# Expert outputs scattered to their tokens' rows, and a combination that loads rows in order

## The chip, the cores and the metric

The kernel runs on one core of a Trainium2 chip. The metric is the device time of one execution in microseconds (us), the median of several runs. The core has five engines that run side by side and wait for each other through semaphores: TensorE (PE in the profile; PEld is its weight load), VectorE (DVE), ScalarE (ACT), GpSimd (POOL) and SyncE (SP), which here issues most DMAs. GpSimd can issue DMAs too, among them the indirect ones, which take a row number per partition.

## What is computed

Two layers of a gated cross-attention network on x of 16 x 256 tokens with 256 numbers each. The change touches only the last block, a mixture of experts with 8 routed experts, of which each token takes 2, and 2 shared ones:

```python
gates = xf @ router_w + router_b
topv, topi = jax.lax.top_k(gates, TOP_K)                 # TOP_K = 2
probs = jax.nn.softmax(topv, axis=-1)
comb = jnp.einsum('nke,nk->ne', jax.nn.one_hot(topi, E), probs)
h = gelu(jnp.einsum('nd,edh->enh', xf, w1) + b1[:, None, :])
y = jnp.einsum('enh,ehd->end', h, w2) + b2[:, None, :]
moe_out = jnp.einsum('ne,end->nd', comb, y)              # 4096 tokens, D = 256, H = 512
shared_out = (jnp.einsum('snh,shd->nd', sh, sw2) + sb2.sum(0)) / S
out = x + tanh(g) * (shared_out + moe_out)
```

## The kernel before

Four phases follow each other; the last, `phase_moe`, has three stages. Every matmul in float32 precision is done as three passes over a high and a low part (`three_passes`, lines 32 to 34), so each operand has a `_hi` and a `_lo` tile: a copy makes the high part, a subtraction the low one.

**Routing** (`moe_route`): 16 chunks of 256 tokens. The layer norm gives `z`; the gates give each token its two experts and, by a count with matmuls, a place in each expert's region of the DRAM tensor `d_z_rows`. GpSimd scatters each token's `z` row to its two places with 64 indirect DMAs (line 2502). Small tables on VectorE say for each of the 39 tiles of 256 rows which expert it belongs to and at which row it starts (`tiles_at`), and for each token and choice where its result will stand (`pos`). The first shared expert runs in this stage too.

**Expert tiles** (`moe_experts`): a software pipeline over 39 tiles (`PAIR_TILES`), written as one order of parts for all engines:

```python
ORDER = (("load_w", 3), ("begin", 1), ("split_w", 2), ("load", 4), ("turn_in", 2), ("first", 1), ("second", 0))
```

In step n an engine does its share of `load_w` for tile n+3, of `begin` for tile n+1, and so on. SyncE loads weights (`load_w`) and stores results (`second`, line 2980). GpSimd copies the weights' high part (`split_w`, a small COPY at line 2993 and the CAST at 2994) and loads the tile's rows (`load`, line 3003). VectorE makes the weights' low part (`split_w`, line 3059), the low part of the turned tokens (`turn_in`, line 2941), the low parts of the hidden values (`begin` and `first`, line 3068) and the sum with the bias (`second`, `ys`, line 3089). TensorE transposes the tile (`turn_in`, line 2951, four matmuls) and multiplies 24 + 24 times. Steps 3 to 34 are a loop in the program of two steps per turn; each engine runs its own instructions in order. A buffer number `u` is the tile's number modulo 2. `load` on GpSimd is:

```python
alone(pool, zt_done, i - 1, passed)
row = pool.value_load(M.tiles_at[:, 1, bass.ds(i, 1)], min_val=0, max_val=(E + 1) * S.ROWS - TOK)
pool.dma_start(z[u][:], z_rows[bass.ds(row, TOK), :].rearrange("(t p) d -> p t d", p=P)).then_inc(z_loaded[u], 16)
```

`alone` waits for a semaphore; `value_load` reads a row number into a register of the sequencer (line 3002). Semaphores that matter: `zt_done` counts transposed tiles, `w_hi_done` and `w_lo_done` the split weights, `gelu_lo` the low parts of hidden values, `y_copied` the finished `ys`, `stored` the DMAs that have emptied a `ys` buffer.

**Combination** (`moe_combine`): 16 chunks again. The second shared expert is computed (`hidden`, `outputs`), and each chunk's 512 expert results are gathered from `d_y_rows` by four indirect DMAs on GpSimd (line 3205) into `rows`, weighed and added to `x_all` by VectorE (`weigh`, line 3244), whose sum with the shared output goes out. VectorE's order is hidden of chunk n, `weigh(n - 1)`, outputs of chunk n - 1.

## Time and profile before

| | |
|---|---|
| median of 3 runs | 1186.05 us (1181.33 to 1189.27) |
| span of the profiled execution | 1181.6 us |
| what lies around the span (median less span) | 4.4 us |
| routing stage | to about 825 us |
| expert tiles | about 825 to 1066 us |
| combination | 1066 us to the end |
| TensorE busy in the whole span | 1096.0 us (93%) |
| VectorE, ScalarE, GpSimd busy | 874.2, 698.7, 442.7 us |

The profiled execution has no other time of its own than its span, from its first to its last instruction. The median of the runs stands beside it, and the difference is what a forecast made in the span's time has to be given back. Busy time doesn't say what bounds a stage; that is read from who waits for whom in it.

### The profile page before, as it was taken

How to read it: one execution, taken by the hardware profiler on the slowest of the kernel's cores; microseconds unless marked ns; L12 is line 12 of the kernel's file. 1: busy time of each engine (PE TensorE's matmuls, PEld its weight loads, DVE VectorE, ACT ScalarE, POOL GpSimd, SP SyncE). 2: the span in 40 equal slices, each digit the busy share in tenths (PEclk: the TensorE clock that was granted, in tenths of full speed). 3: DMA queues.
4: the chain of work that ended last, by engine and by line, in shares of the span. 5: the costliest groups of instructions: out<-in, count | busy, mean ns of one | idle time of the engine just before them, and what ended most of it. 6: DMA issues, size and time to landing. Idle time of an engine off the chain costs nothing. (4 is left out here: it accounts for less than half of the span.)

```text
span 1181.6 us, 28194 instructions
## 1 busy us (share of the span) xinstructions
PE 1096.0 (93%) x9246; PEld 943.8 (80%) x9247; DVE 874.2 (74%) x1984; ACT 698.7 (59%) x1584; POOL 442.7 (37%) x577
## 2 busy tenths in 40 slices
PE   6599988999988999999998798899999999998998
PEld 4366667898976777777775598888999999997987
DVE  8799997766667888888887386476676666664665
ACT  3599975646543676667766543266655555563453
POOL 4278865522201110212100037563423332324664
PEclk9689999999998999999999977889999999998999
DMA  9666621000035454554531167665455455544664
GB/s 320 198 233 218 220 71 54 1 0 0 0 56 123 97 127 88 105 106 88 127 76 38 39 219 256 246 227 201 162 178 171 161 174 169 178 152 143 217 197 140
DMA packets 98895, 164.81 MB, mean 139 GB/s; under 512 B 12140, under 2 KB 73420, under 8 KB 96620
## 3 DMA queue, kind: packets, MB, share of 16 engines
q1 hardware_dynamic: 88988, 136.75, 39.3%
q0 software_dynamic: 9104, 26.49, 6.8%
q8 instruction: 56, 0.92, 0.3%
q10 hardware_dynamic: 704, 0.30, 0.1%
q14 instruction: 43, 0.35, 0.1%
HBM read 103.76 MB, written 33.69 MB: 116 GB/s over the span
## 5 line engine op out<-in xcount | busy, mean ns | idle before, releaser
L1924 DVE TENSOR_REDUCE c_mx<-d_bank 128x2 f32<-128x512 f32 x256 | 164.3, 685 | 14.1 <-PE d_bank L2078 13.6
L1839 ACT ACTIVATE c_probs<-c_t 128x512 f32<-128x512 f32 x248 | 134.7, 598 | 25.1 <-PE c_t L2104 24.3
L3037 ACT ACTIVATE d_g_full<-d_bank,d_e_bias 128x256 f32<-128x256 f32 x156 | 77.2, 495 | 99.9 <-PE d_bank L34 99.9
L32 PE MATMUL d_bank<-de_zt_hi,d_e_hi 128*128 128x256 f32 x312 | 91.8, 294 | 2.4 <-DVE de_zt_lo L2941 2.4
L33 PE MATMUL d_bank<-de_zt_lo,d_e_hi 128*128 128x256 f32 x312 | 88.4, 283 | 0.0
L34 PE MATMUL d_bank<-d_w_hi,d_g_lo 128*128 x312 | 88.2, 283 | 0.0
L33 PE MATMUL d_bank<-d_w_lo,d_g_hi 128*128 x312 | 88.2, 283 | 0.0
L32 PE MATMUL d_bank<-d_w_hi,d_g_hi 128*128 x312 | 88.1, 283 | 0.0
L34 PE MATMUL d_bank<-de_zt_hi,d_e_lo 128*128 128x256 f32 x312 | 87.9, 282 | 0.0
L1765 POOL CAST c_ct_hi<-c_c_raw 128x512 fp32r<-128x512 f32 x15 | 9.2, 611 | 205.4 <-PE c_misc L34 205.4
L3205 POOL DMA_INDIRECT d_w_lo<-d_y_rows,d_pos x64 | 66.6, 1040 | 51.2 <-ACT d_g_hi L3218 19.8
L32 PE MATMUL d_bank<-d_s_hi,d_g_hi 128*128 128x256 f32 x256 | 76.9, 300 | 3.2 <-DVE d_g_lo L3237 1.8
L33 PE MATMUL d_bank<-d_s_lo,d_g_hi 128*128 128x256 f32 x256 | 75.8, 296 | 2.5 <-issue 2.5
L3038 ACT ACTIVATE d_g_hi<-d_bank,d_e_bias 128x256 fp32r<-128x256 f32 x156 | 77.9, 500 | 0.0
L34 PE MATMUL d_bank<-d_s_hi,d_g_lo 128*128 128x256 f32 x256 | 75.7, 296 | 1.7 <-issue 1.7
L3068 DVE TENSOR_TENSOR d_g_lo<-d_g_full,d_g_hi 128x256 fp32r<-128x256 f32 x156 | 70.6, 490 | 7.4 <-ACT d_g_hi L3038 5.3
L3089 DVE TENSOR_TENSOR de_ys<-d_bank,de_out_bias 128x512 f32<-128x512 f32 x39 | 27.0, 692 | 60.3 <-PE d_bank L34 58.2
L2104 PEld LDWEIGHTS c_t<-c_qt,c_kt 50*128 50x128 f32 x496 | 37.2, 185 | 43.0 <-ACT c_probs L1839 21.1
L1504 PE MATMUL b_y<-b_w,b_g_hi 128*128 128x288 f32 x256 | 70.3, 301 | 0.3 <-DVE b_g_lo L1337 0.3
L2116 PE MATMUL c_o<-c_probs,c_va 128*32 128x256 f32 x1024 | 68.5, 385 | 1.0 <-ACT c_probs L1839 1.0
L1505 PE MATMUL b_y<-b_w,b_g_lo 128*128 128x288 f32 x256 | 68.9, 296 | 0.0
L2502 POOL DMA_INDIRECT d_z_rows<-dr_z,dr_pos_i x56 | 57.4, 1025 | 30.3 <-ACT d_g_hi L2544 15.4
(430 smaller groups left out, 3803.1 us busy)
## 6 DMA issues: line engine op xcount, KB each, us to landing
d_e_raw<-in_w SPq DMA_DIRECT2D x39, 514.0 KB, 3.7
a_mb<-a_maxima SPq DMA_DIRECT2D x15, 1024.0 KB, 7.5
d_w_hi<-d_zt_kept SPq DMA_DIRECT2D x26, 512.0 KB
d_y_rows<-de_ys SPq DMA_DIRECT2D x39, 256.0 KB, 2.1
d_z_in<-d_z_rows POOLq DMA_DIRECT2D x37, 256.0 KB, 3.6
c_kt<-c_k_hi SPq DMA_DIRECT2D x64, 128.0 KB, 3.1
c_qt<-c_q_hi SPq DMA_DIRECT2D x64, 128.0 KB, 3.7
d_zt_kept<-d_w_hi SPq DMA_DIRECT2D x20, 256.0 KB
```

Source lines behind the costliest of these rows:

```text
L32: tensor.matmul(out, lhs_hi, rhs_hi, start=start, stop=False)
L33: tensor.matmul(out, lhs_hi, rhs_lo, start=False, stop=False)
L34: return tensor.matmul(out, lhs_lo, rhs_hi, start=False, stop=stop)
L1504: pe.matmul(y[t][:, 0:WIDE], g_hi[:, m, cols], w2[:, m, :], start=(m == 0), stop=False)
L1505: return pe.matmul(y[t][:, 0:WIDE], g_lo[:, m, cols], w2[:, m, :], start=False, stop=(m == KF - 1))
L1839: act.activation(probs[h % PR][:], t_bank(n, p, k), ACT.Exp).then_inc(exp_done, 1)
L1924: dve.tensor_reduce(mx[n % 2][:, :, k, p:p + 1], s_ps[h % SB], AX.X, ALU.max).then_inc(max_done, 1)
L2116: mm = pe.matmul(o_ps[OSLOT * i:OSLOT * (i + 1), g % 2, :], va[n % R][:, j, h, :], probs[(n * H + h) % PR][:, j, :], start=(j == 0), stop= ...
L3037: act.activation(g_full[:, m, :], hid[m][:, 0:TOK], ACT.Gelu, bias=bias[u][:, m:m + 1]).then_inc(gelu_full, 1)
L3038: act.activation(g_hi[u][:, m, :], hid[m][:, 0:TOK], ACT.Gelu, bias=bias[u][:, m:m + 1]).then_inc(gelu_hi, 1)
L3068: dve.tensor_tensor(g_lo[u][:, m, :], g_full[:, m, :], g_hi[u][:, m, :], ALU.subtract).then_inc(gelu_lo, 1)
L3205: pool.indirect_dma_start(rows[n % RR][:, t * TOP + k, :], None, y_rows, bass.IndirectOffsetOnAxis(ap=M.pos[:, T * n + t, k:k + 1], axis=0 ...
```

## The change

The expert tiles no longer store their results in the order of the tiles. Each `z` row in DRAM is two numbers longer (258 instead of 256): the number of the pair row where its result belongs, plus one, and the token's first expert. The tile's rows bring both along. VectorE works out, in `turn_in`, the row in `d_y_rows` for each of the tile's 256 results (`to_row`): the token's number times 2, plus 0 or 1 by whether this tile's expert is the token's first; padding rows go to spare rows. GpSimd then writes `ys` with two indirect DMAs per tile (`scatter`), a step later than SyncE stored it. In the combination the results of a chunk lie in the order of the tokens, and SyncE loads them with one plain DMA per chunk; GpSimd has no part in it. The `z` load stays on GpSimd and gets a second wait. `share_bias` moves ahead of GpSimd's pipeline, and the loops of VectorE and GpSimd hold four steps per turn.

```diff
 class RoutedRows:
+    D = 256
+    WIDE = D + 2
...
-    z_rows = nc.dram_tensor("d_z_rows", [(S.E + 1) * S.ROWS, S.D], F32, kind="Internal").ap()
-    y_rows = nc.dram_tensor("d_y_rows", [S.PAIR_TILES * S.TOK, S.D], F32, kind="Internal").ap()
+    z_rows = nc.dram_tensor("d_z_rows", [(S.E + 1) * S.ROWS, S.WIDE], F32, kind="Internal").ap()
+    y_rows = nc.dram_tensor("d_y_rows", [S.PAIRS + S.PAIR_TILES * S.TOK, S.D], F32, kind="Internal").ap()
...
         pool.memset(above[:], 1.0).then_inc(pool_ready, 1)
-        pool.memset(zeros[:], 0.0).then_inc(zeros_set, 1)
+        pool.memset(zeros[:, :, 0:D], 0.0).then_inc(zeros_set, 1)
+        pool.memset(zeros[:, :, D:D + 1], 2.0 * (S.PAIRS + S.PAIR_TILES * TOK)).then_inc(zeros_set, 1)
+        pool.memset(zeros[:, :, D + 1:], -1.0).then_inc(zeros_set, 1)
+        pool.iota(M.spare_rows[:], pattern=[[TOK, S.PAIR_TILES], [P, T]], base=S.PAIRS, channel_multiplier=1,
+                  allow_small_or_imprecise_dtypes=True).then_inc(tokens_set, 1)
+        for first, count in ((0, routed.TILES), (routed.TILES, TILES - routed.TILES)):
+            pool.iota(z_cols(first, count, D), pattern=[[2 * P, count], [0, 1]], base=2 * P * first + 1, channel_multiplier=2,
+                      allow_small_or_imprecise_dtypes=True).then_inc(tokens_set, 1)
...
         def mark(g):
             step(dve.tensor_copy(top_f[:], top_i[:, :, 0:TOP]))
+            begun = max(0, routed.TILES - GT * g)
+            if begun > 0:
+                dve.tensor_copy(z_cols(GT * g, begun, D + 1), top_i[:, 0:begun, 0:1])
+            step(dve.tensor_copy(z_cols(GT * g + begun, GT - begun, D + 1), top_i[:, begun:, 0:1]))
...
-        def past_regions():
-            for e in range(1, E):
-                dve.tensor_scalar(past_region[:, e], pos_all[:], float(e * S.ROWS), base_step[:, e - 1:e], ALU.is_ge, ALU.mult)
...
-                    dve.tensor_tensor(pos_all[:], pos_all[:], past_region[:, e], ALU.subtract)
...
-        def store(i, u):
+        def load_late(i, u):
...
-            sync.wait_ge(y_copied, i + 1)
-            sync.dma_start(y_rows[bass.ds(i * TOK, TOK), :].rearrange("(t p) d -> p t d", p=P), ys[u][:]).then_inc(stored[u], 16)
...
-        def load(i, u):
+        def load(i, r):
+            u = r % 2
             if prepared(i):
                 return
             alone(pool, zt_done, i - 1, passed)
+            alone(pool, rows_known, i - 1, passed)
             row = pool.value_load(M.tiles_at[:, 1, bass.ds(i, 1)], min_val=0, max_val=(E + 1) * S.ROWS - TOK)
             pool.dma_start(z[u][:], z_rows[bass.ds(row, TOK), :].rearrange("(t p) d -> p t d", p=P)).then_inc(z_loaded[u], 16)
-            if isinstance(i, int) and i == AHEAD:
-                share_bias()
+
+        def scatter(i, r):
+            alone(pool, rows_known, i + 1, passed)
+            alone(pool, y_copied, i + 1, passed)
+            for t in range(T):
+                pool.indirect_dma_start(y_rows, bass.IndirectOffsetOnAxis(ap=to_row[r][:, t:t + 1], axis=0), ys[r % 2][:, t, :],
+                                        None).then_inc(stored[r % 2], 16)
...
-        pipeline(pool, S.PAIR_TILES, ORDER, {"split_w": split_w, "load": load})
+        share_bias()
+        pipeline(pool, S.PAIR_TILES, (("split_w", 2), ("load", 4), ("scatter", -1)), {"split_w": split_w, "load": load, "scatter": scatter}, per=OR)
...
+        def turn_in(i, r):
+            u = r % 2
             if not turned_before(i):
                 turn_dve(dve, i, u)
+            if prepared(i):
+                dve.wait_ge(M.z_in_loaded[u], 16)
+            else:
+                dve.wait_ge(z_loaded[u], before_last(i, u))
+            after(dve, rows_known, i)
+            dve.tensor_tensor(chosen[:], z[u][:, :, D + 1], M.tile_expert[:, bass.ds(i, 1)].broadcast_to([P, T]), ALU.is_equal).then_inc(chosen_done, 1)
+            dve.wait_ge(chosen_done, 2 * i + 1)
+            after(dve, stored[u], 2 * before_last(i, u) - 16 * T)
+            dve.tensor_tensor(chosen[:], z[u][:, :, D], chosen[:], ALU.subtract).then_inc(chosen_done, 1)
+            dve.wait_ge(chosen_done, 2 * i + 2)
+            dve.tensor_tensor(to_row[r][:], chosen[:], M.spare_rows[:, bass.ds(i, 1), :].rearrange("p i t -> p (i t)"), ALU.min).then_inc(rows_known, 1)
...
+    pairs = y_rows[0:S.PAIRS, :].rearrange("(t p k) d -> p t k d", p=P, k=TOP)
...
+        def load_rows(n):
+            after(sync, weighed, T * TOP * (n - RR + 1))
+            sync.dma_start(rows[n % RR].rearrange("p (t k) d -> p t k d", t=T), pairs[:, T * n:T * (n + 1)]).then_inc(gathered[n % RR], 16)
...
-                for k in range(TOP):
-                    pool.indirect_dma_start(rows[n % RR][:, t * TOP + k, :], None, y_rows,
-                                            bass.IndirectOffsetOnAxis(ap=M.pos[:, T * n + t, k:k + 1], axis=0)).then_inc(gathered[n % RR], 16)
```

```order
L2993 COPY d_e_bias<-d_e_raw 128x4
L2994 CAST d_e_hi<-d_e_raw 128x1024
L46 REGISTER_ALU
L3002 ISA
L3002 TENSOR_LOAD d_tiles_at
L3002 ISA x2
L3003 ISA
L3003 DMA d_z_in<-d_z_rows 128x2x256
```

The same step of GpSimd in the changed kernel:

```order
L3016 COPY d_e_bias<-d_e_raw 128x4
L3017 CAST d_e_hi<-d_e_raw 128x1024
L46 REGISTER_ALU
L3027 ISA
L3027 TENSOR_LOAD d_tiles_at
L3027 ISA x2
L3028 ISA
L3028 DMA d_z_in<-d_z_rows 128x2x258
L3034 DMA d_y_rows<-de_ys,de_to_row 18176x256 x2
```

Two indirect DMAs stand between the load and the next step's copies, and the row number is read behind one more wait.

VectorE in the same loop before, from the weights' low part (d_e_lo) by the turned tokens' (de_zt_lo) to the first of three low parts of hidden values (d_g_lo):

```order
L3059 TENSOR_TENSOR d_e_lo<-d_e_raw,d_e_hi 128x1024
L2940 REGISTER_ALU
L2941 TENSOR_TENSOR de_zt_lo<-d_bank,de_zt_hi 128x512
L3066 REGISTER_ALU
L3068 TENSOR_TENSOR d_g_lo<-d_g_full,d_g_hi 128x256
```

The same piece of VectorE in the changed kernel:

```order
L3091 TENSOR_TENSOR d_e_lo<-d_e_raw,d_e_hi 128x1024
L2964 REGISTER_ALU
L2965 TENSOR_TENSOR de_zt_lo<-d_bank,de_zt_hi 128x512
L3100 REGISTER_ALU
L3102 ISA
L3102 TENSOR_TENSOR de_chosen<-d_z_in,d_tile_expert 128x2
L3103 ISA
L40 ISA
L3105 TENSOR_TENSOR de_chosen<-d_z_in,de_chosen 128x2
L3106 REGISTER_ALU
L3107 ISA
L3107 TENSOR_TENSOR de_to_row<-de_chosen,d_spare_rows 128x2
```

Three operations on two numbers per partition have come between, the last of which raises `rows_known`.

GpSimd at the start of the stage before, where the first load of a tile's rows stands ahead of the shared bias:

```order
L3002 TENSOR_LOAD d_tiles_at
L3002 ISA x2
L3003 ISA
L3003 DMA d_z_in<-d_z_rows 128x2x256
L3011 TENSOR_TENSOR de_out_bias<-de_out_bias 128x256
L3013 TENSOR_SCALAR de_out_bias<-de_out_bias 128x256
L3020 TENSOR_TENSOR de_out_bias<-de_out_bias 128x256 x4
```

And in the changed kernel, where it stands behind:

```order
L3041 TENSOR_TENSOR de_out_bias<-de_out_bias 128x256
L3043 TENSOR_SCALAR de_out_bias<-de_out_bias 128x256
L3050 TENSOR_TENSOR de_out_bias<-de_out_bias 128x256 x4
L3027 TENSOR_LOAD d_tiles_at
L3027 ISA x2
L3028 ISA
L3028 DMA d_z_in<-d_z_rows 128x2x258
```

The six operations on the bias have changed places with the load.

## Rows read from the trace of the kernel before

**Rows 1.** The page's first line.

```profile
span 1181.6 us, 28194 instructions
```

**Rows 2.** Busy time by stretch: expert loop, combination; then clock, DMA share, GB/s.

```profile
838.60:1052.80 214.20, 214.20 (x1810) 214.20 (x1810) 145.33 (x245) 121.56 (x312) 66.35 (x105) 1.00 0.53 176
1066.00:1182.00 116.00, 100.34 (x770) 97.86 (x768) 66.69 (x150) 50.08 (x128) 66.57 (x64) 0.92 0.55 172
```

**Rows 3.** The chain's shares: expert loop, then combination.

```profile
by line: PE d_bank L33 31.2%; PE d_bank L34 31.1%; PE d_bank L32 31.1%; PE d_bank L2951 6.8%
...
by line: PE d_bank L34 29.2%; PE d_bank L33 28.0%; PE d_bank L32 27.9%; issue 8.8%; another core or an unknown queue 1.2%; ACT d_g_full L3217 0.4%; DVE x_all L3256 0.4%; ACT d_g_hi L3218 0.4%; DVE d_g_lo L3237 0.4%; ACTq L2269 0.3%; DVEq L3
```

**Rows 4.** TensorE's transposes: timeline of three tiles, and the line's summary.

```profile
830.16 0.60 PE L2951 MATMUL d_bank<-ident,d_z_in 128*128 128x128 f32 x4
...
842.49 0.60 PE L2951 MATMUL d_bank<-ident,d_z_in 128*128 128x128 f32 x4
...
928.73 0.60 PE L2951 MATMUL d_bank<-ident,d_z_in 128*128 128x128 f32 x4
...
L2951 PEld LDWEIGHTS d_bank<-ident,d_z_in x156: 138/140/226, 818.2 to 1052.2; 128*128 128x128 f32 x156
```

**Rows 5.** Busy time by stretch in the combination; columns as in rows 2.

```profile
1082.00:1086.00 4.00, 1.68 (x5) 1.35 (x5) 0.42 (x1) 0.31 (x1) 2.27 (x3) 0.50 0.39 113
```

**Rows 6.** GpSimd's gathers in the combination: the line's summary, then the timeline.

```profile
L3205 POOL DMA_INDIRECT d_w_lo<-d_y_rows,d_pos x64: 942/1008/1222, 1070.1 to 1169.9; - x64
...
1071.41 0.98 POOL L3205 DMA_INDIRECT d_w_lo<-d_y_rows,d_pos  x1 [0.30 <-issue]
1072.69 0.95 POOL L3205 DMA_INDIRECT d_w_lo<-d_y_rows,d_pos  x1 [0.30 <-issue]
1073.94 0.95 POOL L3205 DMA_INDIRECT d_w_lo<-d_y_rows,d_pos  x1 [0.30 <-issue]
```

**Rows 7.** Timeline of GpSimd in the expert loop.

```profile
929.59 0.18 POOL L2993 COPY d_e_bias<-d_e_raw 128x4 f32<-128x4 f32 x1 [4.10 <-DMA d_e_raw<-in_w]
929.72 1.04 POOL L2994 CAST d_e_hi<-d_e_raw 128x1024 fp32r<-128x1024 f32 x1
931.04 0.71 POOL L3003 DMA_DIRECT2D d_z_in<-d_z_rows  x1 [0.29 <-issue]
```

**Rows 8.** Timeline of VectorE in the expert loop.

```profile
929.81 1.23 DVE L3068 TENSOR_TENSOR d_g_lo<-d_g_full,d_g_hi 128x256 fp32r<-128x256 f32 x1
930.95 1.21 DVE L3059 TENSOR_TENSOR d_e_lo<-d_e_raw,d_e_hi 128x1024 fp32r<-128x1024 f32 x1
932.09 0.68 DVE L2941 TENSOR_TENSOR de_zt_lo<-d_bank,de_zt_hi 128x512 fp32r<-128x512 f32 x1
932.69 1.08 DVE L3068 TENSOR_TENSOR d_g_lo<-d_g_full,d_g_hi 128x256 fp32r<-128x256 f32 x3
```

**Rows 9.** Timeline of VectorE, chained small operations of the routing's tables.

```profile
804.08 0.19 DVE L2691 TENSOR_TENSOR dr_tab<-dr_tab,dr_past 1x39 f32<-1x39 f32 x1
804.30 0.17 DVE L2692 TENSOR_SCALAR dr_tab<-dr_tab 1x39 f32<-1x39 f32 x1
```

**Rows 10.** Summaries: row-number reads, z loads (ns min/median/max, first and last start).

```profile
L3002 POOLq TENSOR_LOAD <-d_tiles_at x37: 285/289/572, 819.0 to 1040.9; - x37
L3003 POOL DMA_DIRECT2D d_z_in<-d_z_rows x37: 715/717/788, 820.5 to 1042.1; - x37
```

**Rows 11.** Timeline of GpSimd, start of the expert stage.

```profile
824.01 2.80 POOL L3020 TENSOR_TENSOR de_out_bias<-de_out_bias 128x256 f32<-128x256 f32 x4
```

**Rows 12.** Timeline of TensorE: matmuls at half the clock.

```profile
1088.35 0.41 PE L32 MATMUL d_bank<-d_w_hi,d_sw_hi 128*128 128x256 f32 x1
1088.56 0.41 PE L33 MATMUL d_bank<-d_w_hi,d_sw_hi 128*128 128x256 f32 x1
```

**Rows 13.** Timeline of VectorE: the last `ys`, the first weighing.

```profile
1066.89 0.69 DVE L3089 TENSOR_TENSOR de_ys<-d_bank,de_out_bias 128x512 f32<-128x512 f32 x1 [1.06 <-PE d_bank L34]
...
1076.70 1.87 DVE L3244 SCALAR_TENSOR_TENSOR x_all<-d_w_lo,d_prob,x_all 128x256 f32<-128x256 f32 x4 [3.34 <-DMA d_w_lo<-d_y_rows,d_pos]
```

More of the change, by code:

```diff
@@ L79, in __call__, with pipeline @@
             alone(self.engine, self.semaphore, self.base + self.step, self.passed)
-def pipeline(engine, count, order, parts, head=3):
+def pipeline(engine, count, order, parts, head=3, per=2):
     offsets = [offset for _, offset in order]
-    loops = (count - max(offsets) - head) // 2
+    loops = (count - max(offsets) - head) // per
     def step(n, u):
@@ L90, in step @@
             if name in parts and not (isinstance(n, int) and not 0 <= n + offset < count):
-                parts[name](n + offset, (u + offset) % 2)
+                parts[name](n + offset, (u + offset) % per)
     for n in range(-max(offsets), head):
-        step(n, n % 2)
+        step(n, n % per)
     with engine.Fori(0, loops) as i:
-        for k in range(2):
-            step(2 * i + (head + k), (head + k) % 2)
-    for n in range(head + 2 * loops, count - min(offsets)):
-        step(n, n % 2)
+        for k in range(per):
+            step(per * i + (head + k), (head + k) % per)
+    for n in range(head + per * loops, count - min(offsets)):
+        step(n, n % per)
 class Mlstm:
@@ L2281, in phase_moe @@
             b1 = sb("b1", [P, S.NE, S.KF])
-            z_in = [sb(f"z_in{u}", [P, S.T, S.D]) for u in range(2)]
+            z_in = [sb(f"z_in{u}", [P, S.T, S.WIDE]) for u in range(2)]
             e_raw = [sb(f"e_raw{u}", [P, S.KD * S.FF + S.KF]) for u in range(2)]
@@ L2309, in _ @@
             experts.gpsimd(pool)
-            combine.gpsimd(pool)
         @block.scalar
@@ L2355, in z_tile, with z_row, z_cols @@
     def z_tile(i):
+        return z_row(i)[:, 0:D]
+    def z_row(i):
         return routed.z[:, i, :] if i < routed.TILES else z[:, i - routed.TILES, :]
+    def z_cols(first, count, col):
+        tiles = routed.z[:, first:first + count] if first < routed.TILES else z[:, first - routed.TILES:first - routed.TILES + count]
+        return tiles[:, :, col:col + 1]
     TURNED_AT = (None, None, 4, 5, 6, 7)
@@ L2902, in moe_experts @@
     ys = sb("ys", [P, T, D])
+    OR = 4
+    chosen, to_row = one("chosen", [P, T]), [one(f"to_row{r}", [P, T], mybir.dt.int32) for r in range(OR)]
     out_bias = one("out_bias", [P, S.NE, D])
@@ L2984, in on_sync, with split_w @@
         sync.dma_start(out_bias[:], b2_in.rearrange("e d -> (e d)").partition_broadcast(P).rearrange("p (e d) -> p e d", e=S.NE)).then_inc(bias_loaded, 16)
-        pipeline(sync, S.PAIR_TILES, ORDER, {"load_w": load_w, "second": store})
+        pipeline(sync, S.PAIR_TILES, ORDER, {"load_w": load_w, "second": load_late})
     def on_gpsimd(pool):
-        def split_w(i, u):
+        def split_w(i, r):
+            u = r % 2
             if prepared(i):
@@ L3054, in on_vector, with split_w @@
     def on_vector(dve):
-        def split_w(i, u):
+        def split_w(i, r):
+            u = r % 2
             if prepared(i):
@@ L3068, in low_part, with begin, first @@
             dve.tensor_tensor(g_lo[u][:, m, :], g_full[:, m, :], g_hi[u][:, m, :], ALU.subtract).then_inc(gelu_lo, 1)
-        def begin(i, u):
-            low_part(i, u, 0)
-        def first(i, u):
+        def begin(i, r):
+            low_part(i, r % 2, 0)
+        def first(i, r):
             for m in range(1, KF):
-                low_part(i, u, m)
+                low_part(i, r % 2, m)
         def split_last(k, low, raw, high):
@@ L3079, in split_last, with second @@
             dve.tensor_tensor(low[:], raw, high[:], ALU.subtract).then_inc(last_lo, 1)
-        def second(i, u):
+        def second(i, r):
+            u = r % 2
             if isinstance(i, int) and i == LAST_TILE - 2:
@@ L3091, in second @@
                 split_last(1, M.s2_lo, s2_raw, M.s2_hi)
-        pipeline(dve, S.PAIR_TILES, ORDER, {"begin": begin, "split_w": split_w, "turn_in": turn_in, "first": first, "second": second})
+        pipeline(dve, S.PAIR_TILES, ORDER, {"begin": begin, "split_w": split_w, "turn_in": turn_in, "first": first, "second": second}, per=OR)
     def on_tensor(pe):
@@ L3187, in on_sync @@
             load(n)
+        for u in range(2):
+            sync.wait_ge(experts.stored[u], 16 * T * ((S.PAIR_TILES + 1 - u) // 2))
+        for n in range(2):
+            load_rows(n)
         for n in range(CHUNKS):
@@ L3195, in on_sync @@
         sync.wait_ge(x_stored, 16 * (CHUNKS - 1 + T))
-    def on_gpsimd(pool):
-        for u in range(2):
-            pool.wait_ge(experts.stored[u], 16 * ((S.PAIR_TILES + 1 - u) // 2))
-        for n in range(CHUNKS):
-            after(pool, weighed, T * TOP * (n - RR + 1))
-            for t in range(T):
-                after(pool, gelu_hi, KF * n + (KF // T) * (t if n < LAST else 0) - 1)
-                for k in range(TOP):
-                    pool.indirect_dma_start(rows[n % RR][:, t * TOP + k, :], None, y_rows,
-                                            bass.IndirectOffsetOnAxis(ap=M.pos[:, T * n + t, k:k + 1], axis=0)).then_inc(gathered[n % RR], 16)
     def on_scalar(act):
```

55 lines of the change are left out of this document (31 added, 24 removed).

## The prediction

> **What bounds the kernel now.** I read the page first for the span [rows 1], then the stage table, then the chain of waits inside each stage. The changed code lives in the last phase, which has three stages: routing (to about 825 us), the loop over expert tiles, and the combination (from 1066 us). In the expert loop TensorE is busy in all of the 214.2 us of the steady part, at the full granted clock, and the chain consists of nothing but its instructions [rows 2, 3]. Its transposes of tile 4 start at 842.49 us and those of tile 38 at 1052.2 us, so a tile costs (1052.2 - 842.49) / 34 = 6.17 us [rows 4]. VectorE (145.3 us) and GpSimd (66.4 us) have room on average. The combination runs from 1066 us to the end, 115.6 us, and here TensorE has pauses: 8.8% of the chain is "issue", that is, nothing that the profile shows [rows 3]. That is 0.088 x 115.6 = 10.2 us, and after the longest run of them the granted clock is 0.50, which is the 1.2 GHz level [rows 5]. They stand beside the gathers: GpSimd issues them back to back at 1.25 to 1.28 us each [rows 6], and the expert loop, which has none, has no such pause.
>
> **What the change does to the expert loop.** This is the term that decides, so I follow one step n on GpSimd and VectorE, with the durations of now.
>
> Before, GpSimd's step is: split of the weights of tile n+2, then the load of tile n+4, then nothing until the next weights have landed (4.10 us idle [rows 7]). The load waits for TensorE's transposes alone, which are early. After, the load also waits for `rows_known`, which VectorE's `turn_in` of tile n+2 raises in the same step n, and two scatters follow the load. VectorE's `turn_in(n+2)` stands behind its `split_w(n+2)`, which waits for GpSimd's `split_w(n+2)`. So a ring closes: GpSimd's cast, VectorE's split, its turn, its three small operations, GpSimd's load, two scatters, GpSimd's next cast. Each step holds exactly one turn of it. What is queued behind the waiting load on GpSimd is the next cast, and who waits for that is VectorE and then TensorE's `begin`, by `w_lo_done`.
>
> The ring, from rows: (a) start of the z load to start of the first scatter: 0.72 + 0.30 = 1.02 us [rows 6, 7], the load's duration and the gap ahead of an indirect DMA. (b) First to second scatter 1.25, and the second lasts 0.95 [rows 6]; both are taken from the gathers, since the scatters of the routing are of the same kind. (c) Then COPY: no row has it behind an indirect DMA; between 0 and the 0.30 gap, I take 0.10. COPY to CAST 0.13, CAST 1.04 [rows 7]. (d) End of CAST at 930.76 to VectorE's split at 930.95: 0.19; split to turn 1.14, turn to what follows 0.60 [rows 8]. (e) The three small operations on 128x2 numbers, each waiting for the one before. Chained operations of 1x39 follow each other at 0.21 us, so three take 0.61 [rows 9]; the new ones also compute a register between wait and issue, which no row prices there. I take 0.80, bounds 0.6 and 1.0. (f) From the wait's release to the start of the z load: GpSimd's sequencer must read the tile's row number after the wait. The first and the last of these reads start at 819.0 and 1040.9 us, and their DMAs at 820.5 and 1042.1 us, so 1.5 and 1.2 us [rows 10]. The release of the wait comes on top, for which the 0.19 of (d) is the nearest: 1.4 us, bounds 1.25 and 1.7. Today this time hides behind the cast, which runs meanwhile; behind the new wait nothing hides it.
>
> Sum: 1.02 + 1.25 + 0.95 + 0.10 + 0.13 + 1.04 + 0.19 + 1.14 + 0.60 + 0.80 + 1.40 = 8.62 us, against 6.17 us. TensorE would be idle for 2.45 us of each step. The low bounds give 8.62 - 0.1 - 0.2 - 0.15 = 8.2 us. At the high end stand the longest indirect DMA (1.22 instead of 0.95, twice, [rows 6]), 0.2 more in (c) and in (e) and 0.3 more in (f): 9.9 us, which I don't expect all together; 9.2 is half way.
>
> How often: the first turn begins with the cast of tile 3 in step 1, and the load stands in the steps up to n = 34. That makes 34 turns, 34 x 2.45 = 83 us. Now VectorE's split of a tile ends at 930.95 + 1.21 = 932.16 us [rows 8] and TensorE begins that tile six matmuls of 0.12 us ahead of its next transposes, at 928.73 + 6.17 - 0.72 = 934.2 us [rows 4]: 2 us of slack, used up first. That leaves 81 us. In the last steps there is no load, the ring is open, and TensorE's own 48 matmuls of 214.2 / 1810 = 0.12 us, 5.8 us per tile, set the pace [rows 2].
>
> Everything else in the loop I cost at nothing. SyncE loses the store, so weight loads leave earlier than now. The scatter of a tile is issued a step before its `ys` buffer is wanted, about 8 us where the direct store lands in 2.1. The three small operations (0.8 us of VectorE) fit: it has 69 us free of 214 [rows 2]. The z load leaves 3.9 us into the turn and lands some 3.6 us later, wanted a step on. Cover gone, each of these would lengthen the step by its own time.
>
> **The start of the expert stage.** `share_bias` now stands ahead of the first z load on GpSimd: six operations that run from the end of that load, at 820.5 + 0.79, to 824.01 + 2.80 us, so 5.5 us [rows 10, 11]. Tile 2 is then asked for at about 827 us instead of 820.5 and lands near 831, where TensorE turns it at 830.16 [rows 4]. I take +1 us, bounds 0 and 3.
>
> **Routing.** Rows of 1,032 bytes instead of 1,024, two small copies per group on VectorE, three short iotas on GpSimd, against seven products and seven subtractions of 0.2 us less [rows 9]. No row prices a row length other than 1,024 bytes; from the 0.8% of bytes to the 3 us that the whole load of a tile takes. I take 0, bounds -1 and +3.
>
> **The combination.** 64 gathers go; SyncE loads 512 KB per chunk in one DMA. If TensorE's pauses belong to the gathers, 10 us of pauses go, and with them what the half clock costs, where a matmul follows the last at 0.21 us instead of 0.12 [rows 12]; the mean clock of 0.92 over 116 us [rows 2] is a loss of 9 us at most, part of which the pauses hold already, and I count 4. If they belong to the traffic as such they stay, and four loads now start together. And the first chunk still waits for a chain: last `ys`, two scatters (2.5 us), landing, then a 512 KB load, about 10 us where the trace has 9.1 (from 1066.89 + 0.69 to 1076.70) [rows 13]. Bounds 0 and -14; I take -10, near the pauses, since in 214 us of loop with 0.53 of DMA share there is none.
>
> **A rule beside the rows.** VectorE's subtraction of 128x256 lasts 1.23 us beside GpSimd's cast and 0.36 apart (three in 1.08) elsewhere [rows 8], so these two engines do hold each other up; three of the same stand beside a gather of 0.98 us, where its neighbours have 0.95 [rows 6]. The Trainium skill, "SBUF — State Buffer", section "Who interferes with whom", says that a VectorE instruction with two SBUF inputs contends with a GpSimd instruction that reads SBUF. By that rule the first pair of rows is expected; applied to the scatters, which read their row numbers, it would make the ring longer, and the gather's row speaks against it.
>
> **Rivals.** (1) The ring is hidden, and the kernel is faster: it decides at 6.17 us. Then only the combination counts: 1181.6 - 10 + 1 = 1172.6, with what lies around the span 1177. For it speaks the idle time of GpSimd and VectorE; against it that 8.2 is the sum of the low ends. 0.04. (2) The ring is shorter, 7.2 us, if the register work runs ahead and scatters are issued without gaps: 34 x 1.03 = 35, -2 + 1 - 10 = +24, 1210. 0.10. (3) The ring is longer. Either the scatters and the three subtractions of 0.36 us exclude each other (34 x 1.08 = +37, so 1295), or the clock drops in TensorE's pauses, as it does after those of [rows 5]: at 0.21 us a tile's 48 matmuls take 10.1 us and no longer fit into 8.62, and if half the steps ran so, 17 x 1.5 = +25 stand on top, 1283, if all do, 1308. I take 1300 for the case. 0.11. (4) The change does what it says but the pauses of the combination stay: the forecast plus 10, inside its range. That it doesn't do what it says I leave out: the program's rows show both.
>
> **How the numbers follow.** The profile gives no time for its execution but the span, 1181.6 us; the median of the runs is 4.4 us more, and I carry that. 1181.6 + 81 + 1 + 0 - 10 = 1253.6, and with 4.4 us 1258 us. Its own range: ring 8.2 (34 x 2.03 - 2 = 67) with -14 gives 1239; ring 9.2 (34 x 3.03 - 2 = 101) with 0 and +5 gives 1292; chance 0.75. For 8 times in 10 the range must reach into (2) and (3): 1215 to 1300. A measurement of this kernel tells a change from none at about 1%, that is 12 us. Faster by more than that: 0.02; within: 0.04, from (1) and its surroundings; slower: 0.94.
>
> **What would show it.** In the expert loop of the changed profile: steps of 8.2 to 9.2 us between TensorE's transposes; its `begin` waiting for VectorE's d_e_lo; VectorE's d_e_lo waiting for GpSimd's cast; GpSimd's z load waiting for VectorE's de_to_row for several us; no wait of GpSimd for d_e_raw. The combination shorter by about 10 us, without "issue" pauses. The forecast is wrong if those steps are 6.2 us, or if GpSimd starts the z load less than 0.5 us after de_to_row.

## The result and the profile after

The changed kernel takes 1248.97 us (median of 4 runs, 1247.07 to 1260.81) against 1187.66 us (4 runs, 1181.33 to 1189.77). The ratio is 1.054, with a 95% interval of 1.049 to 1.060: slower. The forecast was 1258 us, within 1215 to 1300. One of the four runs of kernel 1 below was slow (1677.27 us, at a granted clock of 0.556) and is not counted, so its median is 1171.56 us and not the 1172.6 us that later expectations name.

The page's first line, beside [rows 1]:

```profile
span 1247.0 us, 28490 instructions
```

Busy time by stretch, expert loop from the transposes of tile 4 to those of tile 38, then combination (columns as in [rows 2]):

```profile
850.10:1138.40 288.30, 243.27 (x1770) 236.50 (x1769) 147.27 (x339) 123.56 (x306) 135.38 (x171) 0.91 0.41 127
1152.80:1247.00 94.20, 89.75 (x767) 89.55 (x765) 66.64 (x150) 48.60 (x128) 3.40 (x4) 0.99 0.62 213
```

The matmuls of 34 tiles, which filled the 209.4 us from 842.49 to 1051.93 us before, take 288.3 us, and TensorE, which was never idle there, has 45 us without a matmul and a mean clock of 0.91. The combination took 115 us and now takes 94; its chain has no "issue" worth naming any more (0.6%, against the 8.8% of [rows 3]).

TensorE's transposes, the line's summary (beside the last line of [rows 4]):

```profile
L2975 PE MATMUL d_bank<-ident,d_z_in x156: 270/273/447, 823.9 to 1138.7; 128*128 128x128 f32 x156
```

Tile 4 is turned at 850.12 us and tile 38 at 1138.40, so a tile costs 288.3 / 34 = 8.48 us. Who waited for whom in that stretch (us in total, times, longest):

```profile
POOL d_z_in L3028 <- issue: 130.4, 33, 4.8
DVE d_e_lo L3091 <- POOL d_e_hi L3017: 124.7, 34, 4.6
...
PE d_bank L32 <- DVE de_zt_lo L2965: 45.0, 33, 2.3
```

Two engines wait for each other in a circle, GpSimd ahead of its z load and VectorE for GpSimd's cast, and TensorE waits for VectorE, outside the circle. One turn of it, on GpSimd and then on VectorE (beside [rows 7, 8]):

```profile
960.32 0.77 POOL L3028 DMA_DIRECT2D d_z_in<-d_z_rows  x1 [3.93 <-issue]
961.39 1.01 POOL L3034 DMA_INDIRECT d_y_rows<-de_ys,de_to_row  x1 [0.30 <-issue]
962.71 0.97 POOL L3034 DMA_INDIRECT d_y_rows<-de_ys,de_to_row  x1 [0.30 <-issue]
963.68 0.20 POOL L3016 COPY d_e_bias<-d_e_raw 128x4 f32<-128x4 f32 x1
963.81 1.05 POOL L3017 CAST d_e_hi<-d_e_raw 128x1024 fp32r<-128x1024 f32 x1
968.80 0.77 POOL L3028 DMA_DIRECT2D d_z_in<-d_z_rows  x1 [3.94 <-issue]
...
964.89 1.22 DVE L3091 TENSOR_TENSOR d_e_lo<-d_e_raw,d_e_hi 128x1024 fp32r<-128x1024 f32 x1 [3.51 <-POOL d_e_hi L3017]
966.04 0.68 DVE L2965 TENSOR_TENSOR de_zt_lo<-d_bank,de_zt_hi 128x512 fp32r<-128x512 f32 x1
966.64 0.15 DVE L3102 TENSOR_TENSOR de_chosen<-d_z_in,d_tile_expert 128x2 f32<-128x2 f32 x1
966.92 0.16 DVE L3105 TENSOR_TENSOR de_chosen<-d_z_in,de_chosen 128x2 f32<-128x2 f32 x1
967.21 0.16 DVE L3107 TENSOR_TENSOR de_to_row<-de_chosen,d_spare_rows 128x2 int32<-128x2 f32 x1
```

Read it as a clock: load at 960.32, scatters, copy and cast end at 964.86, split at 964.89, turn, three small operations to 967.37, and the next load at 968.80, 8.48 us after the last. The 3.94 us that GpSimd waits is put down to "issue" and not to `de_to_row`: behind the wait its sequencer reads the row number, and the chain of waits shows the pieces, of which these are the longest.

```profile
967.57 0.29 POOLq L3027
967.86 0.03 issue
967.89 0.15 POOLq L3027
...
968.24 0.54 issue
968.78 0.03 POOLq L46
968.81 0.06 POOL d_z_in L3028
```

Of the 1.43 us between the last small operation and the load, the read takes 0.29, address work 0.15, and 0.54 just ahead of the DMA is time that nothing in the profile explains.

Where the 65.4 us between the two spans (1181.6 and 1247.0) lie: tile 0's transposes come 823.90 - 818.26 = 5.6 us later; from there to tile 4's it is 26.2 us instead of 24.2 (+2.0); tiles 4 to 38 cost 78.9 more; from the last transposes to the end it is 108.6 us instead of 129.7 (-21.1).

### The profile page after: what moved, and what is told of

Read it like the earlier page. It is cut to its first block and busy times, and to the rows that moved or that the text cites. A ratio compares the mean times of both kernels' runs of the same rounds, so it can differ in the third digit from the quotient of the medians.

```text
span 1247.0 us, 28490 instructions
## 1 busy us (share of the span) xinstructions
PE 1117.9 (90%) x9246; PEld 960.6 (77%) x9247; DVE 883.7 (71%) x2092; ACT 701.8 (56%) x1584; POOL 456.6 (37%) x596
## 5 line engine op out<-in xcount | busy, mean ns | idle before, releaser
L32 PE MATMUL d_bank<-de_zt_hi,d_e_hi 128*128 128x256 f32 x312 | 105.0, 337 | 46.5 <-DVE de_zt_lo L2965 46.4
L3091 DVE TENSOR_TENSOR d_e_lo<-d_e_raw,d_e_hi 128x1024 fp32r<-128x1024 f32 x37 | 47.9, 1295 | 126.4 <-POOL d_e_hi L3017 126.4
L32 PEld LDWEIGHTS d_bank<-de_zt_hi,d_e_hi 128*128 128x128 f32 x312 | 68.9, 221 | 53.6 <-issue 49.0
L33 PE MATMUL d_bank<-de_zt_lo,d_e_hi 128*128 128x256 f32 x312 | 96.9, 311 | 0.0
L34 PE MATMUL d_bank<-de_zt_hi,d_e_lo 128*128 128x256 f32 x312 | 96.6, 310 | 0.0
L3034 POOL DMA_INDIRECT d_y_rows<-de_ys,de_to_row x78 | 79.9, 1025 | 30.6 <-issue 24.5
L3028 POOL DMA_DIRECT2D d_z_in<-d_z_rows x37 | 28.4, 766 | 139.7 <-issue 139.0
L2515 POOL DMA_INDIRECT d_z_rows<-dr_z,dr_pos_i x56 | 57.8, 1032 | 35.9 <-ACT d_g_hi L2564 19.0
```

Source lines behind the costliest of these rows:

```text
L32: tensor.matmul(out, lhs_hi, rhs_hi, start=start, stop=False)
L33: tensor.matmul(out, lhs_hi, rhs_lo, start=False, stop=False)
L34: return tensor.matmul(out, lhs_lo, rhs_hi, start=False, stop=stop)
L2515: pool.indirect_dma_start(z_rows, bass.IndirectOffsetOnAxis(ap=pos_i[:, at:at + 1], axis=0), z_row(i), None).then_inc(scattered[2 * i // T ...
L3034: pool.indirect_dma_start(y_rows, bass.IndirectOffsetOnAxis(ap=to_row[r][:, t:t + 1], axis=0), ys[r % 2][:, t, :], None).then_inc(stored[r ...
L3091: dve.tensor_tensor(w_lo[u][:], w_raw[u][:, 0:KD * FF], w_hi[u][:], ALU.subtract).then_inc(w_lo_done, 1)
```

## The experiments

Twelve kernels ran, each timed against the kernel before on the same chip. "Tile" is the mean time between TensorE's transposes over tiles 4 to 38, "tail" the time from the last transposes to the end of the span, both of the profiled run.

| kernel | median us | ratio to before (95%) | tile us | tail us |
|---|---|---|---|---|
| before | 1187.7, 1184.6, 1185.6 in the three groups | 1 | 6.16 | 129.7 |
| changed | 1248.97 | 1.049 to 1.060 | 8.48 | 108.6 |
| 1: z load on SyncE | 1171.56 | 0.986 to 0.990 | 6.19 | 108.1 |
| 2: scatters ahead of the load | 1174.98 | 0.987 to 0.992 | 6.22 | 108.6 |
| 3: rows computed early | 1177.82 | 0.990 to 0.995 | 6.36 | 108.2 |
| 4: row number read ahead of the waits | 1229.12 | 1.033 to 1.037 | 7.87 | 108.6 |
| 5: kernel 1 with gathers again | 1195.52 | 1.007 to 1.014 | 6.18 | 131.0 |
| 6: kernel 1, rows in 1 KB pieces | 1170.12 | 0.981 to 0.992 | 6.23 | 108.8 |
| 7: kernel 1, rows loaded by GpSimd | 1170.17 | 0.982 to 0.992 | 6.18 | 108.2 |
| 8: before, z rows of 1,032 bytes | 1183.46 | 0.996 to 1.002 | 6.12 | 126.5 |
| 9: kernel 1, TensorE's stage written out | 1169.16 | 0.984 to 0.991 | 6.19 | 108.2 |
| 10: before, TensorE's stage written out | 1183.72 | 0.997 to 1.002 | 6.16 | 126.3 |
| 11: a third scatter per tile | 1294.55 | 1.090 to 1.098 | 9.77 | 110.4 |
| 12: kernel 8 with the two fields filled | 1183.80 | 0.998 to 1.002 | 6.13 | 127.2 |

**The ring, cut in three places.** Kernel 1 gives the load to SyncE, in its own order of parts:

```diff
+            after(sync, zt_done, i - 1)
+            after(sync, rows_known, i - 1)
+            row = sync.value_load(M.tiles_at[:, 1, bass.ds(i, 1)], ...)
+            sync.dma_start(z[u][:], z_rows[bass.ds(row, TOK), :]...).then_inc(z_loaded[u], 16)
...
-{"split_w": split_w, "load": load, "scatter": scatter}
+{"split_w": split_w, "scatter": scatter}
```

> The load of the tile's z rows is issued by SyncE instead of GpSimd, with the same two waits; nothing else changes. Ring theory (GpSimd's cast, VectorE's split and rows, GpSimd's load, its scatters, its next cast): the ring is cut, GpSimd's step holds only 1.2 + 2.5 us of work, and a tile costs TensorE's 6.17 us again instead of 8.48, so 34 x 2.3 = 78 us less than the changed kernel's 1249: 1171 us, between TensorE's transposes steps of 6.2. Rival, contention (the scatters slow VectorE, or hold the weight loads up): the step stays above 7.5 us and the time above 1215.

Measured: 1171.56 us, a tile every 6.19 us. Kernel 2 changes one line, GpSimd's order:

```diff
-(("split_w", 2), ("load", 4), ("scatter", -1))
+(("split_w", 2), ("scatter", -1), ("load", 4))
```

> In each step GpSimd issues its two scatters ahead of the load of z rows instead of behind it; the same instructions otherwise. Ring theory: the scatters (2.5 us) then run while GpSimd would wait for rows_known, and the ring is 8.47 - 2.5 = 6.0 us, just under TensorE's 6.17: 1171 us, up to 1182 if the step is 6.5. Rival, GpSimd has too much work or its DMA issues contend: the order doesn't matter, 1235 to 1250.

Measured: 1174.98 us. The instructions are the same, their number and their engines too, and 74 us are gone. The casts from 1028.47 to 1052.45 us follow each other at 6.0 us, just under TensorE's 6.16. GpSimd's timeline shows two kinds of such steps, one from 1040.45 us and one from 1046.45 us:

```profile
1041.67 1.98 POOL L3034 DMA_INDIRECT d_y_rows<-de_ys,de_to_row  x1 [0.17 <-issue]
1045.55 0.76 POOL L3028 DMA_DIRECT2D d_z_in<-d_z_rows  x1 [0.63 <-issue]
...
1047.67 1.02 POOL L3034 DMA_INDIRECT d_y_rows<-de_ys,de_to_row  x1 [0.17 <-issue]
1051.55 0.76 POOL L3028 DMA_DIRECT2D d_z_in<-d_z_rows  x1 [1.59 <-issue]
```

In the second the load stands 1.47 us behind `de_to_row` (1050.08 us): that is the ring, 8.48 us less the 2.5 of the scatters. In the first a scatter of 1.98 us fills the room, and GpSimd's own work follows itself without a longer wait than 0.63 us. The trace shows no reason why both come to 6.0 us. Kernel 3 takes the third way, VectorE's three small operations ahead of its split:

```diff
-    OR = 4
+    OR = 8
...
-pipeline(dve, S.PAIR_TILES, ORDER, {...}, per=OR)
+pipeline(dve, S.PAIR_TILES, ORDER[0:2] + (("rows_of", 2),) + ORDER[2:], {..., "rows_of": rows_of}, head=7, per=OR)
```

> VectorE computes a tile's rows (the three small operations) ahead of its split of the weights in the same step, with eight buffers of rows instead of four so that no scatter is waited for; GpSimd's order is the changed kernel's. Ring theory: rows_known no longer hangs on the cast, the ring is open, step 6.2 us, 1171 us. Rival, the second wait costs by itself (register work behind a wait on GpSimd, wherever it stands): step 7.3 us or more, 1208 or more.

Measured: 1177.82 us. GpSimd's order is that of the changed kernel and its second wait is there, so neither costs the 2.3 us a tile by itself; that the wait hung on the cast did. A tile takes 6.36 us here, 0.2 more than TensorE needs. VectorE's timeline of kernel 3, and the load that follows on GpSimd, show why:

```profile
972.35 0.21 DVE L3105 TENSOR_TENSOR de_chosen<-d_z_in,d_tile_expert 128x2 f32<-128x2 f32 x1
972.59 0.16 DVE L3108 TENSOR_TENSOR de_chosen<-d_z_in,de_chosen 128x2 f32<-128x2 f32 x1
972.88 1.66 DVE L3110 TENSOR_TENSOR de_to_row<-de_chosen,d_spare_rows 128x2 int32<-128x2 f32 x1
974.55 1.23 DVE L3091 TENSOR_TENSOR d_e_lo<-d_e_raw,d_e_hi 128x1024 fp32r<-128x1024 f32 x1
...
975.96 0.77 POOL L3028 DMA_DIRECT2D d_z_in<-d_z_rows  x1 [1.45 <-issue]
```

The third small operation, 0.16 us in the changed kernel, lasts 1.66. Meanwhile GpSimd's second scatter (to 973.33), its copy and its cast (973.46 to 974.51 us) follow each other without a gap, and the small operation ends at 974.54, just after the cast. So no semaphore ties `rows_known` to the cast any more, but this hold does: in 24 steps of the loop one of the small operations is held until a cast ends, the load starts 1.4 us behind the last of them, and the next cast ends about 4.8 us after that. This is a shorter ring, mostly of 6.2 and 6.5 us in turn, and TensorE's steps go with it, 6.3 and 6.4 us in turn. What holds the operation from 972.88 us until the cast begins at 973.46 is open, since the two ahead of it take 0.21 and 0.16 us beside the same scatter.

**The ring's terms.** Kernel 4 moves one line of the load up:

```diff
+            row = pool.value_load(M.tiles_at[:, 1, bass.ds(i, 1)], ...)
             alone(pool, zt_done, i - 1, passed)
             alone(pool, rows_known, i - 1, passed)
-            row = pool.value_load(M.tiles_at[:, 1, bass.ds(i, 1)], ...)
```

> GpSimd reads the tile's row number ahead of the two waits of the z load instead of behind them. Ring theory, term (f): of the 1.4 us from the wait's release to the DMA's start some 1.2 leave the ring, 8.47 - 1.2 = 7.3 us a step, 34 x 1.2 = 41 us less: 1208 us. If the time after the wait is not the reading but the issue of the DMA itself, nothing changes: 1245 to 1250.

Measured: 1229.12 us, half of what was expected; a tile takes 7.87 us. GpSimd's row of kernel 4, where `de_to_row` ends at 960.34 us:

```profile
961.13 0.77 POOL L3028 DMA_DIRECT2D d_z_in<-d_z_rows  x1 [3.30 <-DVE de_to_row L3107]
```

From 960.34 to 961.13 it is 0.79 us, against 1.43 with the read behind the wait. In 33 of 34 turns of kernel 4 it is 0.75 to 0.80 us. So the read and its address work are 0.64 us of the ring's term (f), the time from the wait's release to the load, and the other 0.79 us pass with nothing left to read. Kernel 11 lengthens the ring with a DMA to a tensor that nobody reads:

```diff
+            pool.indirect_dma_start(y_copy, bass.IndirectOffsetOnAxis(ap=to_row[r][:, 1:2], axis=0), ys[r % 2][:, 1, :],
+                                    None).then_inc(stored[r % 2], 16)
```

> The changed kernel with a third indirect DMA per tile, which writes the second half of ys a second time, to a tensor that nobody reads. Ring theory: GpSimd's time between load and next cast grows by one scatter, 1.3 us, and so does the step, from 8.48 to 9.8: 34 x 1.32 = 45 us more than 1249, 1294. Rival, the step is set by something else (the landing of the weights, the clock): 1249 to 1260.

Measured: 1294.55 us; a tile takes 9.77 us, 1.29 more. GpSimd's timeline shows the third DMA at the others' distance, 1.28 us:

```profile
1007.09 1.01 POOL L3035 DMA_INDIRECT d_y_rows<-de_ys,de_to_row  x1 [0.30 <-issue]
1008.41 0.97 POOL L3035 DMA_INDIRECT d_y_rows<-de_ys,de_to_row  x1 [0.30 <-issue]
1009.69 0.97 POOL L3037 DMA_INDIRECT d_y_copy<-de_ys,de_to_row  x1 [0.30 <-issue]
1010.65 0.21 POOL L3017 COPY d_e_bias<-d_e_raw 128x4 f32<-128x4 f32 x1
```

What GpSimd does between load and cast thus costs its own length once per tile. Kernel 4 shows the same for what is taken out of the ring, 0.64 us out of a turn and 0.61 off a tile.

**The combination.** It gained 21 us where I had said 10. Three kernels on the base of kernel 1 ask what in the fetching of the rows was dear. Kernel 5 takes the loads from SyncE and gives GpSimd the gathers of the kernel before, with an index that runs in order:

```diff
+        pool.iota(M.pos[:], pattern=[[TOP * P, S.TILES], [1, TOP]], base=0, channel_multiplier=TOP, ...)
...
+                    pool.indirect_dma_start(rows[n % RR][:, t * TOP + k, :], None, y_rows[0:S.PAIRS, :],
+                                            bass.IndirectOffsetOnAxis(ap=M.pos[:, T * n + t, k:k + 1], axis=0)).then_inc(gathered[n % RR], 16)
```

> The kernel with the z load on SyncE (1172.6 us), but its combination fetches each chunk's rows again with four indirect DMAs per 256 tokens from GpSimd, paced as in the kernel before; the rows still lie in the order of the tokens, so only the way of fetching differs. Theory: TensorE's pauses and its half clock in the combination come from the gathers, and the 21 us by which that stage got shorter come back: 1193 us, with issue pauses. Rival, the stage is shorter because the rows lie in order (whoever fetches them): 1173 us, no pauses.

Measured: 1195.52 us, 24.0 us above kernel 1 and 25.4 above kernels 6 and 7, which belong to its group. The tail is 131.0 us long, near that of the kernel before (129.7) and 22.9 more than kernel 1's. TensorE's waits in the combination of kernel 5:

```profile
PE d_bank L34 <- issue: 5.4, 6, 2.2
PE d_bank L32 <- issue: 4.3, 7, 1.0
PE d_bank L33 <- issue: 3.3, 5, 1.0
PE d_bank L32 <- DVE d_g_lo L3297: 2.8, 1, 2.8
```

Kernel 1 has none in its combination, with the same rows in the same order. That is the cause shown: the gathers, not where the rows lie. Busy time by stretch in the combination of kernel 5 and in that of kernel 1 (columns as in [rows 2]):

```profile
1076.00:1193.40 117.40, 97.45 (x774) 94.85 (x772) 67.08 (x151) 50.28 (x128) 69.64 (x69) 0.94 0.54 171
```

```profile
1074.00:1167.80 93.80, 89.88 (x768) 89.67 (x766) 66.47 (x150) 48.43 (x128) 3.38 (x4) 1.00 0.63 214
```

More traffic per us without gathers (214 GB/s against 171) and yet no pause: it isn't the traffic. Kernels 6 and 7 vary the plain loads, in smaller pieces and from GpSimd's queue:

```diff
-            sync.dma_start(rows[n % RR].rearrange("p (t k) d -> p t k d", t=T), pairs[:, T * n:T * (n + 1)])...
+            for t in range(T):
+                for k in range(TOP):
+                    sync.dma_start(rows[n % RR][:, t * TOP + k, :], pairs[:, T * n + t, k, :])...
```

```diff
-            sync.dma_start(rows[n % RR].rearrange("p (t k) d -> p t k d", t=T), pairs[:, T * n:T * (n + 1)])...
+            pool.dma_start(rows[n % RR].rearrange("p (t k) d -> p t k d", t=T), pairs[:, T * n:T * (n + 1)])...
```

> The same kernel with the z load on SyncE, each chunk's rows loaded by SyncE in four plain DMAs of 1 KB pieces instead of one of 2 KB pieces. Theory, pauses belong to GpSimd's indirect DMAs: 1173 us, none of the pauses. Rival, they belong to many small packets on the DMA engines: pauses come back, 1180 to 1193.

> The same kernel with the z load on SyncE, each chunk's rows loaded by one plain DMA issued by GpSimd. Theory, the indirect kind makes the pauses: 1173 us, up to 1175. Rival, everything that GpSimd's DMA queue moves makes them: pauses stand beside 16 loads, 1180 to 1193.

Measured: 1170.12 and 1170.17 us, both with tails of 108 to 109 us and without an issue pause between 1075 us and the end of the combination. So neither pieces of 1 KB on SyncE's queue nor one plain DMA per chunk on GpSimd's makes them, and the 64 indirect DMAs do. Four plain DMAs per chunk from GpSimd were not run, so whether their being indirect or their number on this queue counts is not separated.

But the expert stage of the changed kernel has indirect DMAs too, 78 of them. It runs as a loop, the combination as straight code, so I formed a theory on the supply of instructions. Kernels 9 and 10 write TensorE's part of the stage out for all 39 tiles, with the scatters (on kernel 1) and without (on the kernel before):

```diff
-        pipeline(pe, S.PAIR_TILES, ORDER, {...})
+        pipeline(pe, S.PAIR_TILES, ORDER, {...}, head=35)
```

> The kernel with the z load on SyncE (1172.6 us), with TensorE's instructions of the expert stage written out for all 39 tiles instead of as a loop; the other engines keep their loops. Theory, indirect DMAs hold up the supply of instructions to an engine that runs straight code: the 78 scatters then make pauses in the expert stage as the 64 gathers did in the combination (21 us, 0.33 us each), up to 26 us: 1180 to 1198. Rival, a pause needs the gathers' own density or direction: 1172, no pauses.

> The kernel before with TensorE's instructions of the expert stage written out in the same way; there are no indirect DMAs in this stage. Theory: no pauses, the time of the kernel before, 1184 to 1188. Rival, straight code pauses by itself: 1195 or more, with issue pauses in the expert stage.

Measured: 1169.16 and 1183.72 us, tiles of 6.19 and 6.16 us, no issue pause in the expert stage of either. The theory that indirect DMAs hold up straight code in general falls. What remains differs in two ways: the gathers come every 1.25 us in bursts of several and move data into SBUF, the scatters come two per 6.2 us and move it out.

A trace of the kernel before bears on this, though no run varies it alone. Its routing, written out too, has 64 indirect DMAs, and they are scatters: 52 of them from 702.35 to 782.18 us, most of them 1.3 to 1.5 us apart. TensorE's waits from 702 to 785 us, and the summary of most of these scatters:

```profile
PE d_bank L2791 <- issue: 2.4, 2, 1.2
PE d_bank L33 <- issue: 2.3, 5, 0.9
PE d_bank L32 <- issue: 2.2, 4, 1.0
...
L2502 POOL DMA_INDIRECT d_z_rows<-dr_z,dr_pos_i x56: 956/962/1658, 716.2 to 804.2; - x56
```

All its lines together are 20 pauses and 11.3 us. From 650 to 702 us, without an indirect DMA, there is none, and none from 785 to 840 us, where the last 12 scatters come in fours with 1 to 3 us between the fours. So data that leaves SBUF goes with such pauses as well, and how densely the DMAs come is what the traces point to.

**The routing.** Tile 4's transposes stand at 842.5, 846.9, 844.4 and 842.8 us in the before, 8, 10 and 12, and between 848.1 and 852.1 us (mean 850.4) in the ten traces with the changed routing and start of the stage. So 6 us are real. The first transposes take most of that, 820.5 against 825.6 us on average. Kernel 8 widens the z rows of the kernel before, kernel 12 fills the two fields as well:

```diff
-        self.z = sb("z0", [P, self.TILES, 256], F32)
+        self.z = sb("z0", [P, self.TILES, 258], F32)
...
+            step(dve.tensor_copy(z_cols(GT * g + begun, GT - begun, D + 1), top_i[:, begun:, 0:1]))
```

(the second added line is kernel 12's, with the two iotas of the change).

> The kernel before, with z rows of 1,032 bytes instead of 1,024 in SBUF and DRAM (two zeros behind each row), nothing else. Theory: the 5.6 us by which the routing stage got longer come from the row length: first transposes of the expert stage near 824 instead of 818.3 us, time 1193. Rival, they come from the new small operations or the order in routing: 1187 to 1188, first transposes near 818.

> The kernel before with z rows of 1,032 bytes and with the two fields filled as in the changed kernel: two iotas on GpSimd, one or two small copies on VectorE in each group of the routing. Theory, these small operations make the routing 5.6 us longer: first transposes of the expert stage at 823 or later, time 4 to 6 us above the 1183.5 of the same kernel without them. Rival, it is neither (then the tables or the neighbourhood of the next stage): first transposes near 820, 1183 to 1185.

Measured: 1183.46 and 1183.80 us, first transposes at 821.2 and 822.3 us. The row length and the small operations are not it. Nor is it the six operations on the bias: in the changed kernel they begin at 827.21 us, behind the first transposes at 823.90. The delay is older. The last scatter of the routing starts at 804.17 us before and at 810.35 in the changed kernel, and the first transposes stand 12.9 to 15.1 us behind it in all fourteen traces. What remains of the change is the tables, which are now computed on 128 partitions; that they are the cause was not tested.

## Why the prediction was right, step by step

**The ring** (forecast 8.62 us, bounds 8.2 and 9.2; measured 8.48). Term by term, as the prediction lists them, from the turn shown above: load to first scatter 1.07 (1.02 forecast), first to second 1.32 (1.25), second 0.97 (0.95), then COPY at once (0.10), COPY to CAST 0.13 (0.13), CAST 1.05 (1.04), to the split 0.03 (0.19), split to turn 1.15 (1.14), turn to the small operations 0.60 (0.60), these 0.73 (0.80), release to load 1.43 (1.40). Both hand-overs came out near nothing. The first, COPY behind a scatter, had no row. The second, cast to split, was misread: in [rows 8] VectorE is busy with `d_g_lo` until 929.81 + 1.23 = 931.04 us, past the start of its split at 930.95, so the 0.19 us there is VectorE's own work and no hand-over. The same 0.19 us stands in (f) for the wait's release, and has no row there either. Term (f) had the right size and the wrong content: I took it for the reading of the row number almost alone, and kernel 4 gave back 0.61 us a tile where I expected 1.2.

**How often** (34 turns, less 2 us of slack: 81). From the transposes of tile 4 to those of tile 38 it is 78.9 us. Most turns take 8.37 to 8.49 us, and 34 of 8.48 less the slack would give 77. The slack is there, the first of the 34 steps takes 6.48 us, but five turns are 0.4 to 0.9 us longer, such as the cast at 937.63 that is followed by the next at 946.97; they make up for it, for a reason that the traces don't show.

**The start** (+1) was +2.0. **Routing** (0, bounds -1 and +3) was +5.6 and lies outside the bounds (+5.1 by the means of four and ten traces): a term mis-sized, with its cause open, as told above. **The combination** (-10, bounds 0 and -14) was -21.1, also outside. The mechanism was right, kernel 5 shows it, and the size was half: the step that failed is "near the pauses". I counted the issue pauses of the chain (10 us) and 4 us for the half clock, and then took less than their sum, while more than the sum went. By the stretches, TensorE's time without a matmul fell from 15.3 to 4.5 us, 10.8 less, near the pauses indeed, and its busy time on the same matmuls from 100.3 to 89.8 us: the half clock was worth about 10 us, not 4. The time of a stage without the pauses could have been worked out: 768 matmuls of 0.12 us are 92 us, against 115.6 then and 94 now. I should have taken that as the lower end. **What lies around the span** (4.4) was 2.0 in median less span. The 4.4 compared a median with the span of another execution: where runs of the kernel before list both, their time is 2.0 to 2.1 us above their span, and 1.6 in the changed kernel. Together: +5.6 + 1.0 - 2.1 - 11.1 - 2.4 = -9.0, the distance from 1258 to 1248.97. The two terms outside their bounds have opposite signs, and so the total is nearer than they are, which is luck; the ring, which decides the sign, is right without their help.

**Everything else in the loop at nothing**: kernels 1 and 2 confirm it, since with the ring cut a tile takes 6.19 to 6.22 us with all of the new work still in it.

**The rivals.** (1), hidden: no. (2), a shorter ring of 7.2 us: no, GpSimd's scatters are not issued without gaps and the registers don't run ahead, but kernel 4 is a step towards it with 7.87. (3), a longer ring: the clock did drop, to 0.91 in the stage. TensorE's timeline of the changed kernel behind one of its waits:

```profile
940.76 0.38 PE L32 MATMUL d_bank<-de_zt_hi,d_e_hi 128*128 128x256 f32 x1 [2.15 <-DVE de_zt_lo L2965]
940.98 0.28 PE L33 MATMUL d_bank<-de_zt_lo,d_e_hi 128*128 128x256 f32 x1
...
942.50 0.41 PE L33 MATMUL d_bank<-de_zt_lo,d_e_hi 128*128 128x256 f32 x1
942.71 0.41 PE L34 MATMUL d_bank<-de_zt_hi,d_e_lo 128*128 128x256 f32 x1
```

After 2 us without work the matmuls first follow each other at 0.12 us, then at 0.21, the 1.2 GHz level, for a part of the step; a step of 8.48 us has room for that. The other half of (3), that scatters and VectorE's subtractions exclude each other, didn't show in the changed kernel (the turn above has its scatters where VectorE does neither), but it is true of a scatter and VectorE's longer split. The scatters' summary in the changed kernel, and then a scatter of kernel 2, where VectorE's split of the weights runs from 959.72 to 960.95 us:

```profile
L3034 POOL DMA_INDIRECT d_y_rows<-de_ys,de_to_row x78: 966/1007/1990, 850.0 to 1156.3; - x78
```

```profile
959.85 1.99 POOL L3034 DMA_INDIRECT d_y_rows<-de_ys,de_to_row  x1 [0.16 <-issue]
```

Issued just behind the start of a split of the weights, a scatter lasts 1.99 us instead of the median 1.01, which is the rest of the split (1.1) and about the time that it takes alone. In kernel 1, 35 of the 78 scatters are held so, and a tile still takes 6.19 us. The one that begins first is not held: where the scatter of kernel 2 at 1047.67 us leads the split at 1047.71 by 0.04 us, they last 1.02 and 1.22 us, as alone. The prediction weighed the Trainium skill, "SBUF — State Buffer", section "Who interferes with whom", against one gather's row and leaned to the row. Kernels 2 and 3 side with the rule: a scatter that begins second waits for VectorE's subtraction, and in kernel 3 a VectorE operation on two numbers ends only with GpSimd's cast, 1.66 us instead of 0.16, though it begins ahead of it. The measurement decides for the scatters; the gather's row stays as it is.

**What would show it**: steps of 8.48, VectorE's split waiting for the cast (124.7 us in 34 waits), the load 1.43 us behind `de_to_row`, no wait of GpSimd for `d_e_raw`, no pause in the combination. Two were off in the name: TensorE's `begin` is shown as waiting for `de_zt_lo`, which stands behind `d_e_lo` on VectorE and comes last, and GpSimd's load as waiting for "issue", the sequencer's work behind the released wait.

## What to carry to other kernels

A wait that is added to an in-order engine is to be followed around, not along: who sets the semaphore, what that one waits for, and whether the waiting engine's own later work is in that chain. If it is, the turn's sum over all engines, against the bound of the loop, is the forecast; average idle time (GpSimd had 69% of the stage free) says nothing. The repair is then a matter of one line: work that the awaited event doesn't need goes ahead of the wait (kernel 2), or the waiting instruction goes to an engine outside the chain (kernel 1). The same change is then 1.0 to 1.2% faster than before instead of 5% slower. All of that comes from the gathers that went, since with them kernel 5 is 1% slower than before.
